# A two-layer recurrent kernel on one core: the last sequence's value projection moved behind the experts, and two orders swapped

## The chip, the cores and the metric

The kernel runs on one core of a Trainium2 chip. The metric is device time in microseconds (us) of one execution, as the median over runs.

## What is computed

The input is eight sequences of 512 tokens with 128 features, float32. Layer 0 normalises each token, runs causal attention with two query heads and one shared key/value head, and a mixture of eight experts of which each token takes two; the output is x + attention * silu(experts). Layer 1 (a causal convolution, a gated running state, a small memory product and a gated feed-forward) follows on the same rows. Cut to what the change touches:

```python
xn = _layernorm(x)
k = apply_rope(xn @ Wk.T);  v = xn @ Wv.T;  q = apply_rope(einsum(xn, Wq))
w = softmax(where(causal, q @ k.T * scale, -inf))
s = (w @ v) @ Wo.T                      # attention, two heads
g = silu(experts(xn))                   # 8 experts, each token takes the best two
x = x + s * g                           # then layer 1 on x
```

## The kernel before, in words

The kernel names every instruction and orders each engine's queue by hand; engines meet at counting semaphores.

**Order of the stages.** First the normalisation and the router; then attention of sequences 0 to 6; then the experts over 71 tiles of 128 slots (the tokens have been scattered into slots sorted by expert); then attention of sequence 7, for which queries and keys were made before the experts; then layer 1, sequence by sequence. Only the last attention lies between the experts and layer 1.

**Attention of one sequence** (attend, NS = 8 steps, one for each pair of a block of 128 query rows and a head, in the order of STEPS). In step k TensorE does scores(k) (two float32 passes and a small bf16 matmul that adds the causal mask, lines 804 and 806), turn(k-1) (transposes of the exponentials, line 820) and weigh(k-2) (their product with the values, line 842). VectorE takes the row maximum (row_max, line 1330), ScalarE the exponential with its row sum (exponent, line 1796) and copies the transposed tile out of its bank (turned, line 1805), VectorE inverts the row sum (line 1335). For the even outputs ScalarE scales the head-0 product (head0, line 1814), and VectorE adds head 1 to it (combine, line 1323). A weigh of head 1 waits for the head0 copy that reads the same bank. Each engine runs its list in order, so an instruction that waits holds up all that stand behind it.

**Projections of the next sequence** sit in the same steps, at the steps of PROJECT_AT: parts 0 to 2 are queries and keys (line 785) with the rotation on VectorE (lines 1301 to 1313); part 3 is the value projection, four 128x256 products (eight passes, line 792), into banks 1 and 0. ScalarE copies these banks into U with two copies (values, lines 1766 and 1767). For sequence 7, part 3 stands at step 7 of attention 6, and its copies in finish(6), between turned(7) and head0(3). proj_full counts the projections, proj_free the banks that are free again; the experts start once proj_free has reached 4 * (NB + 1) = 32, which includes these copies.

**Experts** (c_step). Per tile TensorE does the gate (line 928), the up (line 937) and, for the tile before, the down product (line 946); ScalarE the gelu (line 1895) and a copy of the next up weights (line 1821); VectorE transposes the next tile's tokens (c_turn, line 1380), forms the product (line 1425), and for the tile before adds the bias (line 1399) and scales into YO (c_out, line 1408). GpSimd scatters YO to rows_y in DRAM (c_send, line 637), two buffers in turn; so c_out(j) waits until the scatter of tile j-2 has landed (c_st). GpSimd's first scatter waits for the slots' tags, which it casts at line 633. SyncE's queue loads the gate weights (line 452) and the token tiles (line 477).

**Last attention.** attend(NB, first=True, last=True), the first of a new pipeline. At step 1 TensorE waits for the last YO and runs keep_warm(0, 5), five 128x512 bf16 matmuls whose result nobody reads (line 736). When all scatters have landed, SyncE issues 16 loads of 256 KB (line 509): for each sequence, the rows of both choices of expert, into Y0 (over XR) and Y1 (over XNT, the normalised input transposed). VectorE starts layer 1 within this attention: d_first_both (line 1463, the sum of the two rows of sequence 0) in step 4 behind row_max and the reciprocal, d_first_product (line 1467) in step 5, d_first_gate with d_add_x (lines 1472, 1502) in step 6, d_stats(0) in step 7. ScalarE's tanh of those sums (d_tanh, line 1930) stands at the end of steps 4 and 6.

Of the kernel before, what the change touches and what calls it, by code (L numbers as in the profile page):

```python
# [27 lines left out]
NSEQ, SEQ = 8, 512  # L28
# [32 lines left out]
def stores(u):  # L61

    return (SLOT_TILES + 1 - u) // 2


NB = NSEQ - 1
# [3 lines left out]
PROJECT_AT = [(1, 3, 5, 7), (1, 4, 6, 7)]  # L70
# [14 lines left out]
def build(nc, t, out):  # L85
    ctx = ExitStack()
    with ctx:
# [3 lines left out]
        def sem(name):  # L91
            return ctx.enter_context(nc.semaphore(name))
# [224 lines left out]
        proj_full = sem("proj_full")  # L317
        proj_free = sem("proj_free")
# [102 lines left out]
        def _(sp):  # L421
# [83 lines left out]
            for u in range(2):  # L505
                sp.wait_ge(c_st[u], 16 * stores(u))
            for b in range(NSEQ):
                for k, y in ((0, Y0), (1, Y1)):
                    sp.dma_start(y[:, b * TPS:(b + 1) * TPS, :], rows_y_t[:, k, b * TPS:(b + 1) * TPS, :]
                                 ).then_inc(rows_in[b], 16)  # L510
# [219 lines left out]
        def _(pe):  # L730
# [3 lines left out]
            def keep_warm(bank, times):  # L734
                for _ in range(times):
                    pe.matmul(B[bank][:].rearrange("p (a b) -> p a b", b=P), ONB[:],
                              ONB[:, None, :].broadcast_to([P, 4, P]), start=True, stop=True)
# [108 lines left out]
            def count():  # L846

                pe.wait_ge(r_m, 1)
                pe.wait_ge(proj_free, 4)
                pe.matmul(B[1][:, NT * E:2 * NT * E], ONB[:], MB, start=True, stop=True)  # L850
                pe.matmul(B[1][:, 0:NT * E], lowb, MB, start=True, stop=True).then_inc(r_cnt, 1)

            def attend(b, u, first=False, last=False):
                for k in range(NS):
                    scores(b, u, k)
                    if b == 0 and k == 1:
                        project(0, 0, 3)
                        turn(0, 0)
                        composite(1)
                        count()  # L860
                    if b == 0 and k == 2:
                        composite(2)
                    if not last and k in PROJECT_AT[b == 0]:
                        project(b + 1, 1 - u, PROJECT_AT[b == 0].index(k))
                    if last and k == 1:
                        pe.wait_ge(c_yo, SLOT_TILES)
                        keep_warm(0, 5)
                    if not (first and k < 1) and not (b == 0 and k == 1):
                        turn(b if k >= 1 else b - 1, (k - 1) % NS)
                    if not (first and k < 2):  # L870
                        weigh(b if k >= 2 else b - 1, u if k >= 2 else 1 - u, (k - 2) % NS)
# [89 lines left out]
                    pe.reg_load(e_down, TEXP[0:1, bass.ds(j - 1, 1)])  # L961
                    c_down(j - 1, 1 - u, pe.snap(e_down, min_val=0, max_val=E - 1))

            pe.wait_ge(proj_free, 4 * (NB + 1))
            for j in range(WBUFS):
                c_step(j, j % 2, j)
            with pe.Fori(1, C_ROUNDS) as i:
# [206 lines left out]
        def _(dve):  # L1174
# [152 lines left out]
            def row_max(b, k):  # L1327
                i, _ = STEPS[k]
                dve.wait_ge(s_full, NS * b + (k + 1))
                dve.tensor_reduce(NM[:, k:k + 1], B[2 + k % 2][:, 0:(i + 1) * P], AX.X, ALU.max,  # L1330
                                  negate=True).then_inc(max_done, 1)
# [4 lines left out]

            def attend(b, u, first=False, last=False):
                for k in range(NS):
                    row_max(b, k)
                    if b == 0 and k == 1:  # L1340
                        choose(1)
                        mark(1)
                    if not (first and k == 0):
                        denominator(b if k else b - 1, (k - 1) % NS)
                    if b == 0 and k == 2:
                        offsets()
                    if b == 0 and k == 3:
                        gates()
                    if last and k == 4:
                        d_first_both()  # L1350
                    if last and k == 5:
                        d_first_product()
                    if k in (5, 6):
                        combine(b, k - 5)
                    if k in (1, 2) and not first:
                        combine(b - 1, k + 1)
                    if k in ROPE_AT[b == 0] and not last:
                        rope_begin(b + 1, ROPE_AT[b == 0].index(k))
                    if k - 1 in ROPE_AT[b == 0] and not last:
                        rope_end(b + 1, 1 - u, ROPE_AT[b == 0].index(k - 1))  # L1360
                    if b == 1 and k in (1, 3, 5):
                        experts((k - 1) // 2)
                    if last:
                        if k == 6:
                            d_first_gate()
                        if k == 7:
                            d_stats(0)
# [93 lines left out]
            def d_first_both():  # L1461
                dve.wait_ge(rows_in[0], 16 * 3)
                dve.tensor_tensor(Y0[:, 0:TPS, :], Y0[:, 0:TPS, :], Y1[:, 0:TPS, :], ALU.add).then_inc(d_mo, 1)
# [261 lines left out]
        def _(act):  # L1725
# [38 lines left out]
            def values(b, u):  # L1764
                act.wait_ge(proj_full, 4 * b + 4)
                act.activation(U[u][:, 0:2, :], B[0][:].rearrange("p (i d) -> p i d", i=2), ACT.Copy)
                act.activation(U[u][:, 2:4, :], B[1][:].rearrange("p (i d) -> p i d", i=2), ACT.Copy
                               ).then_inc(proj_free, 1)
# [30 lines left out]
            def turned(b, k):  # L1799
                i, _ = STEPS[k]  # L1800
                n = NS * b + k
                act.wait_ge(t_done, n + 1)
                if not (isinstance(b, int) and n < 2):
                    act.wait_ge(pv_done, n - 1)
                act.activation(PT[k % 2][:, 0:(i + 1) * P], B[4 + k % 2][:, 0:(i + 1) * P], ACT.Copy  # L1805
                               ).then_inc(pt_done, 1)

            def head0(b, c):
                k = {0: 0, 1: 1, 2: 4, 3: 5}[c]
                n = NS * b + k  # L1810
                act.wait_ge(pv_done, n + 1)
                act.wait_ge(rd_done, n + 1)
                reg = B[6 + k % 2][:, 0:P]
                act.activation(O0[c], reg, ACT.Copy, scale=RD[:, k:k + 1]).then_inc(o0_done, 1)  # L1814
# [14 lines left out]
            def attend(b, u, first=False, last=False):  # L1829
                for k in range(NS):  # L1830
                    if k in (3, 4):
                        head0(b, k - 3)
                    if k == 7:
                        head0(b, 2)
                    if k == 0 and not first:
                        head0(b - 1, 3)
                    if b == NB - 1 and k == 6:
                        first_up_weights(0, e_this)
                    if b == NB - 1 and k == 7:
                        first_up_weights(1, e_next)  # L1840
                    exponent(b, k)
                    if isinstance(b, int) and b == 0 and k == 1:
                        values(0, 0)
                    if not (first and k == 0):
                        turned(b if k else b - 1, (k - 1) % NS)
                    if isinstance(b, int) and b == 0:
                        if k in (1, 2):
                            composite(k)
                        if k == 1:
                            counted()  # L1850
                        if k == 2:
                            exponents()
                        if k >= 4 and k - 4 + KEPT < TAPS:
                            j = k - 4 + KEPT
                            act.activation(TAPW[:, k - 4, :], W3[:, 2, :], ACT.Copy,
                                           scale=VEC[:, V_CONV + j:V_CONV + j + 1]).then_inc(w_am, 1)
                    if last:
                        if k == 4:
                            d_tanh(0)
                        if k == 6:  # L1860
                            d_tanh(1)
                if not last and b != NB - 1:
                    values(b + 1, 1 - u)

            def finish(b):
                turned(b, NS - 1)
                if b == NB - 1:
                    values(b + 1, 1 - b % 2)
                head0(b, 3)
                bring_table(ACT.Gelu if b < NSEQ - 1 else ACT.Silu)  # L1870

            def counted():
# [280 lines left out]
```

## Time and profile before

| what | value |
|---|---|
| median of three runs | 527.14 us (527.08 to 527.35) |
| the profiled execution | 528.09 us, of which its span 526.2 us |
| TensorE matmul busy | 512.3 us, 97% of the span |
| VectorE, ScalarE, GpSimd busy | 390.9, 314.0, 234.6 us |
| attention 6 ends, experts start | at 157.85 us of the span |
| last attention starts | at 348.95 us |

The profile is of one execution; times below are from the start of its span. A row of a timeline gives the start, the duration, the engine, the line and the tile written and read, how many instructions are merged, and in brackets how long the engine sat idle before it and what released it. Durations of matmuls overlap: a float32 product is two passes, and the next pass starts before the modelled end of the one before.

### The profile page before, as it was taken

Reading aid. Unit: us, or ns where it says so; the run is one execution under the profiler, and the core shown is the slowest. Engines: PE = TensorE matmul, PEld = TensorE weight load, DVE = VectorE, ACT = ScalarE, POOL = GpSimd, SP = SyncE. Lnnn points to the kernel's source line nnn. Section 1 sums busy time; section 2 is a strip of 40 time slices with the busy share of each in tenths; the row PEclk is TensorE's granted clock in tenths of the full one; section 3 lists DMA queues with packets and bytes.
Section 4 is the critical chain, followed back from the end, with each engine's and each line's share of the span. In section 5 each row is a group of like instructions: output and inputs, shape, how many; then the busy total and the mean of one; then the engine's idle time right before and its main releaser. Section 6 shows DMA issues by size and latency. Waiting matters only on the chain. (4 is left out here: it accounts for less than half of the span.)

```text
span 526.2 us, 12857 instructions
## 1 busy us (share of the span) xinstructions
PE 512.3 (97%) x3181; PEld 385.9 (73%) x3182; DVE 390.9 (74%) x1107; ACT 314.0 (60%) x830; POOL 234.6 (45%) x244
## 2 busy tenths in 40 slices
PE   9998999999999999999999999998999999999997
PEld 5756677777769999999999999976445545554544
DVE  6589878887776777677777777757788788788654
ACT  5635556556567666666666666657876657656521
POOL 4427766665532333333333333334477646523310
PEclk9999999999999999999999999999999999999999
DMA  8920133345429656555555566419000000000000
GB/s 238 379 109 22 42 102 106 100 127 172 141 43 124 149 146 152 146 149 142 156 137 155 135 152 147 122 55 285 7 0 20 16 5 21 21 0 21 21 19 22
DMA packets 85267, 54.00 MB, mean 103 GB/s; under 512 B 53088, under 2 KB 70016, under 8 KB 85104
## 3 DMA queue, kind: packets, MB, share of 16 engines
q1 hardware_dynamic: 80912, 44.66, 33.7%
q0 software_dynamic: 4320, 8.92, 4.7%
q8 instruction: 16, 0.26, 0.2%
q14 instruction: 19, 0.16, 0.1%
HBM read 37.82 MB, written 15.74 MB: 102 GB/s over the span
## 5 line engine op out<-in xcount | busy, mean ns | idle before, releaser
L1895 ACT ACTIVATE AR<-bank,BGT 128x128 f32<-128x128 f32 x284 | 81.3, 368 | 69.3 <-PE bank L928 69.3
L637 POOL DMA_INDIRECT rows_y<-YO,W1E x71 | 69.0, 972 | 118.6 <-DVE YO L1408 115.4
L1425 DVE SCALAR_TENSOR_TENSOR AR<-bank,B1T,AR 128x128 f32<-128x128 f32 x284 | 80.1, 344 | 3.7 <-ACT AR L1895 2.5
L601 POOL DMA_INDIRECT slots_x<-XR,SLOT x64 | 63.8, 996 | 36.5 <-DMA slots_x<-XR,SLOT 19.9
L946 PE MATMUL bank<-W2E,AR 128*128 x568 | 75.1, 275 | 0.5 <-DVE AR L1425 0.5
L928 PE MATMUL bank<-AR,WGE 128*128 128x128 f32 x568 | 75.1, 275 | 0.0
L937 PE MATMUL bank<-AR,WGE 128*128 128x128 f32 x568 | 75.0, 275 | 0.0
L946 PEld LDWEIGHTS bank<-W2E,AR 128*128 128x128 f32 x568 | 69.1, 192 | 0.7 <-issue 0.7
L937 PEld LDWEIGHTS bank<-AR,WGE 128*128 128x128 f32 x568 | 69.2, 192 | 0.0
L928 PEld LDWEIGHTS bank<-AR,WGE 128*128 128x128 f32 x568 | 69.1, 192 | 0.0
L1796 ACT ACTIVATE AR<-bank,AR 128x512 f32<-128x512 f32 (+1 forms) x64 | 33.8, 528 | 54.0 <-DVE AR L1330 54.0
L842 PE MATMUL bank<-AR 128*128 128x128 f32 x320 | 47.9, 280 | 1.9 <-ACT AR L1814 1.0
L1380 DVE STREAM_TRANSPOSE AR<-XG 128x128 f32<-128x128 f32 x71 | 22.1, 311 | 35.6 <-PE bank L937 27.8
L1330 DVE TENSOR_REDUCE AR<-bank 128x1 f32<-128x512 f32 (+1 forms) x64 | 31.0, 487 | 20.2 <-PE bank L806 19.8
L1821 ACT ACTIVATE WGE<-SPARE 128x512 f32 x71 | 45.5, 641 | 0.3
L804 PE MATMUL bank<-AR 128*128 128x128 f32 (+3 forms) x128 | 45.1, 435 | 0.0
L842 PEld LDWEIGHTS bank<-AR 128*128 128x128 f32 x320 | 40.7, 191 | 5.0 <-ACT AR L1805 3.3
L820 PEld LDWEIGHTS bank<-CST,AR 128*128 128x128 f32 x160 | 19.2, 140 | 23.0 <-ACT AR L1796 11.2
L2027 ACT ACTIVATE W1E<-bank 128x512 f32<-128x512 f32 x32 | 19.0, 593 | 26.9 <-PE bank L1070 26.9
L1070 PE MATMUL bank<-WGE,WGT 128*128 128x512 f32 x64 | 32.7, 593 | 0.7 <-DVE X L1636 0.7
L1076 PE MATMUL bank<-WGE,WUP 128*128 128x512 f32 x64 | 32.7, 592 | 0.0
L1588 DVE SCALAR_TENSOR_TENSOR SPARE<-W2E,VEC,SPARE 128x512 f32<-128x512 f32 x35 | 31.7, 905 | 1.1
(217 smaller groups left out, 907.6 us busy)
## 6 DMA issues: line engine op xcount, KB each, us to landing
WGE<-in_wgu SPq DMA_DIRECT2D x71, 256.0 KB
XG<-slots_x SPq DMA_DIRECT2D x140, 32.0 KB
slots_x<-W1E SPq DMA_DIRECT2D x7, 585.0 KB, 7.3
X<-in_x SPq DMA_DIRECT2D x8, 256.0 KB, 5.6
SPARE<-in_wgu SPq DMA_DIRECT2D x8, 256.0 KB, 2.8
W2E<-in_w SPq DMA_DIRECT2D x8, 256.0 KB, 3.2
XR<-rows_y SPq DMA_DIRECT2D x8, 256.0 KB, 5.3
XNT<-rows_y SPq DMA_DIRECT2D x8, 256.0 KB, 5.4
```

Source lines behind the costliest of these rows:

```text
L601: pool.indirect_dma_start(out=slots_x, out_offset=bass.IndirectOffsetOnAxis(ap=SLOT[:, k, n:n + 1], axis=0), in_=XR[:, n, :], in_offset=No ...
L637: pool.indirect_dma_start(out=rows_y, out_offset=bass.IndirectOffsetOnAxis(ap=DST[:, j:j + 1], axis=0), in_=YO[q % 2][:], in_offset=None). ...
L804: pe.matmul(bank[:, 0:(i + 1) * P], QT[u][h][:, i * P:(i + 1) * P], QT[u][2][:, 0:(i + 1) * P], start=True, stop=False)
L842: mm = pe.matmul(reg, PT[k % 2][:, j * P:(j + 1) * P], U[u][:, j, h * P:(h + 1) * P], start=(j == 0), stop=(j == i))
L928: mm = pe.matmul(B[1 + u][:, c * P:(c + 1) * P], WB[:, q, c * P:(c + 1) * P], XT[u], start=True, stop=True)
L937: mm = pe.matmul(B[3 + u][:, c * P:(c + 1) * P], WU[:, u, c * P:(c + 1) * P], XT[u], start=True, stop=True)
L946: mm = pe.matmul(B[5 + u][:, 0:P], HT[u][:, c, :], W2E[:, bass.ds(e, 1), c, :], start=(c == 0), stop=(c == FC - 1))
L1070: pe.matmul(B[5 - 3 * (c % 2)][:], WGT[:, c * P:(c + 1) * P], H2, start=True, stop=True).then_inc(d_g, 1)
L1425: s = dve.scalar_tensor_tensor(out=HT[u][:, c, :], in0=B[3 + u][:, c * P:(c + 1) * P], scalar=B1T[:, bass.ds(e, 1), c], in1=ZB[u][:, c, :] ...
L1796: act.activation(PR[k % 2][:, 0:(i + 1) * P], B[2 + k % 2][:, 0:(i + 1) * P], ACT.Exp, bias=NM[:, k:k + 1], accum_out=DEN[:, k:k + 1]).the ...
L1821: act.activation(WU[:, u:u + 1, :], SPARE[:, bass.ds(e, 1), :], ACT.Copy).then_inc(c_wu, 1)
L1895: act.activation(ZB[u][:, c, :], B[1 + u][:, c * P:(c + 1) * P], ACT.Gelu, bias=BGT[:, bass.ds(e, 1), c]).then_inc(c_gelu, 1)
```

## The change

TensorE leaves out the last projection of attention 6 and does it in step 1 of attention 7, in place of the five warm matmuls. The experts wait for one count less. ScalarE copies the values in step 1 of attention 7, behind the exponent and ahead of turned(0); in finish(6), head0(3) now stands ahead of turned(7). VectorE's d_first_both moves from behind row_max(4) and the reciprocal to ahead of them. SyncE waits for the last projection before it loads the rows of sequence 7 over XNT.

```diff
@@ sync @@
             for b in range(NSEQ):
+                if b == NSEQ - 1:
+                    sp.wait_ge(proj_full, 4 * NSEQ)
                 for k, y in ((0, Y0), (1, Y1)):
@@ tensor, attend @@
-                    if not last and k in PROJECT_AT[b == 0]:
+                    if not last and k in PROJECT_AT[b == 0] and not (b == NB - 1 and k == 7):
                         project(b + 1, 1 - u, PROJECT_AT[b == 0].index(k))
                     if last and k == 1:
+                        project(b, u, 3)
                         pe.wait_ge(c_yo, SLOT_TILES)
-                        keep_warm(0, 5)
@@ tensor, experts @@
-            pe.wait_ge(proj_free, 4 * (NB + 1))
+            pe.wait_ge(proj_free, 4 * NB + 3)
@@ vector, attend @@
                 for k in range(NS):
+                    if last and k == 4:
+                        d_first_both()
                     row_max(b, k)
...
-                    if last and k == 4:
-                        d_first_both()
@@ scalar, attend and finish @@
                     exponent(b, k)
-                    if isinstance(b, int) and b == 0 and k == 1:
-                        values(0, 0)
+                    if isinstance(b, int) and b in (0, NB) and k == 1:
+                        values(b, u)
...
             def finish(b):
+                if b == NB - 1:
+                    head0(b, 3)
                 turned(b, NS - 1)
-                if b == NB - 1:
-                    values(b + 1, 1 - b % 2)
-                head0(b, 3)
+                if b == NB:
+                    head0(b, 3)
                 bring_table(ACT.Gelu if b < NSEQ - 1 else ACT.Silu)
```

## Rows read from the trace of the kernel before

**Rows 1.** The page, busy time and share of the span by engine

```profile
PE 512.3 (97%) x3181; PEld 385.9 (73%) x3182; DVE 390.9 (74%) x1107; ACT 314.0 (60%) x830; POOL 234.6 (45%) x244
```

**Rows 2.** Timeline of TensorE at the end of attention 6: start, duration, engine, line

```profile
152.24 2.24 PE L792 MATMUL bank<-CVO,XNT 128*128 128x256 f32 x8
154.32 0.49 PE L820 MATMUL bank<-CST,AR 128*128 128x128 f32 x3
...
155.39 0.94 PE L842 MATMUL bank<-AR 128*128 128x128 f32 x6
157.33 0.68 PE L842 MATMUL bank<-AR 128*128 128x128 f32 x4 [1.00 <-ACT AR L1814]
157.85 1.06 PE L928 MATMUL bank<-AR,WGE 128*128 128x128 f32 x8
```

**Rows 3.** Timeline of ScalarE in the same stretch

```profile
154.40 0.47 ACT L1796 ACTIVATE AR<-bank,AR 128x256 f32<-128x256 f32 x1 [0.50 <-DVE AR L1330]
...
154.86 0.48 ACT L1805 ACTIVATE AR<-bank 128x384 f32<-128x384 f32 x1
155.56 0.39 ACT L1805 ACTIVATE AR<-bank 128x256 f32<-128x256 f32 x1 [0.22 <-PE bank L820]
155.85 0.59 ACT L1766 ACTIVATE AR<-bank 128x512 f32<-128x512 f32 x1
...
156.80 0.38 ACT L1814 ACTIVATE AR<-bank,AR 128x128 f32<-128x128 f32 x1
```

**Rows 4.** Timeline of VectorE around the output of expert tile 2

```profile
168.17 0.28 DVE L1399 TENSOR_TENSOR YB<-bank,B2E 128x128 f32<-128x128 f32 x1
168.68 0.29 DVE L1408 TENSOR_SCALAR YO<-YB,W1E 128x128 f32<-128x128 f32 x1 [0.23 <-DMA rows_y<-YO,W1E]
169.63 0.31 DVE L1380 STREAM_TRANSPOSE AR<-XG 128x128 f32<-128x128 f32 x1 [0.66 <-issue]
```

**Rows 5.** Timeline of GpSimd: the first and the last scatter of expert rows

```profile
164.26 1.00 POOL L637 DMA_INDIRECT rows_y<-YO,W1E  x1 [0.61 <-POOL W1E L633]
...
350.23 0.97 POOL L637 DMA_INDIRECT rows_y<-YO,W1E  x1 [0.57 <-DVE YO L1408]
```

**Rows 6.** Timeline of TensorE: the gate product of expert tile 5

```profile
170.39 1.06 PE L928 MATMUL bank<-AR,WGE 128*128 128x128 f32 x8
```

**Rows 7.** Timeline of SyncE's queue: the first two loads of rows

```profile
352.48 0.39 SPq L509 DMA_DIRECT2D XR<-rows_y  x1
352.91 0.51 SPq L509 DMA_DIRECT2D XNT<-rows_y  x1
```

**Rows 8.** Timeline of TensorE in the last attention

```profile
350.20 1.24 PE L736 MATMUL bank<-ONB 128*128 128x512 bf16 x5
351.86 0.66 PE L820 MATMUL bank<-CST,AR 128*128 128x128 f32 x4 [0.42 <-ACT AR L1796]
...
353.38 1.06 PE L842 MATMUL bank<-AR 128*128 128x128 f32 x8
...
355.03 0.66 PE L820 MATMUL bank<-CST,AR 128*128 128x128 f32 x4 [0.31 <-ACT AR L1796]
```

**Rows 9.** Timeline of ScalarE in the last attention

```profile
352.55 0.60 ACT L1805 ACTIVATE AR<-bank 128x512 f32<-128x512 f32 x1 [0.40 <-PE bank L820]
354.20 0.69 ACT L1796 ACTIVATE AR<-bank,AR 128x512 f32<-128x512 f32 x1 [1.05 <-DVE AR L1330]
...
357.24 0.58 ACT L1796 ACTIVATE AR<-bank,AR 128x384 f32<-128x384 f32 x1 [0.67 <-DVE AR L1330]
```

**Rows 10.** Timeline of VectorE in step 4 of the last attention

```profile
356.65 0.56 DVE L1330 TENSOR_REDUCE AR<-bank 128x1 f32<-128x384 f32 x1 [1.48 <-PE bank L806]
...
357.19 0.67 DVE L1463 TENSOR_TENSOR XR<-XR,XNT 128x512 f32<-128x512 f32 x1
```

**Rows 11.** The loads of rows, issue to landing: the first two, then all 16

```profile
DMA to landing us min/median/max: 3.3/3.5/3.8
...
DMA to landing us min/median/max: 3.3/5.4/5.7
```

## The prediction, made before the changed kernel was run

> **What bounds the kernel now.** I read the page's busy times first: TensorE is busy for 97% of the span [rows 1], and the other three are far below. A change of order can win or lose only where TensorE stands still, or by the passes it drops or adds. So I went on to TensorE's timeline at the two seams that the change touches, and from each of its waits to the engine that ended it. At the first seam TensorE idles 1.00 us ahead of the last weigh of attention 6, until ScalarE's head0 copy (line 1814) has read the bank [rows 2]; ScalarE had put the two value copies ahead of that copy [rows 3]. At the second seam, in the last attention, TensorE waits 0.42 us for the first exponential, which is after the five warm matmuls, and 0.31 us for the third [rows 8]. Then I followed what a seam that is earlier runs into: a VectorE instruction that waits for a scatter [rows 4, 5], and the first loads of expert rows [rows 7, 11].
>
> All sums are against the profiled execution, 528.09 us with a span of 526.2, and what they give is carried over to the median of 527.14. A measurement of this kernel can tell about 0.2%, 1.05 us, from no change.
>
> **Leaving attention 6.** The eight passes of line 792 run from 152.24 to the next instruction at 154.32: 2.08 us go from TensorE [rows 2]. They free nothing by themselves. ScalarE's exponential of step 7 starts at 154.40 on VectorE's row maximum, and turned(6) right behind it at 154.86 [rows 3]; neither waits for the projection, so the six passes of weigh that need turned(6) still start at 155.39 [rows 2]. What follows is shorter. Behind turned(6), which ends at 155.34, head0(3) (0.38 us) goes first, as its product is then long made, to about 155.6; turned(7) already starts at 155.56 when nothing is ahead of it and takes 0.39 us [rows 3], so it ends near 155.95. The six passes hand over at about 156.05 (their end of 156.33 less the overlap of 0.16 to 0.3 that modelled ends have here), and the last weigh follows at 156.08 in place of 157.33 [rows 2]. **TensorE reaches the experts 1.25 us earlier**, at 156.60 in place of 157.85. The new wait of the experts asks only for the rotated keys and queries, done before. The gelu table is loaded behind turned(7), 1.2 us earlier too, and stays hidden behind the first gate product of 1.06 us plus the up product.
>
> **What that earlier start collides with.** VectorE's c_out(2) (line 1408) waits for the scatter of tile 0 to land, since both use one YO buffer. It was already a little late: idle 0.23 us, released by that DMA at 168.68 [rows 4]. The scatter was issued at 164.26, as soon as GpSimd had cast the tags [rows 5]; the tags come by a DMA that starts from the end of the token scatter and not from TensorE, so this time doesn't move. Nor does its queue: SyncE issues those loads one behind the other without a pause there. Queued behind c_out(2) on VectorE is c_turn(5), which starts at 169.63 and takes 0.31 us [rows 4], and TensorE's gate product of tile 5 needs it: 170.39 before [rows 6], 169.14 wanted now. With the 0.15 us that lie between a VectorE end and the matmul, it starts at 169.94 + 0.15 = 170.09. **So 0.30 us of the 1.25 is left.** Afterwards VectorE's step is no longer than TensorE's, and nothing is won back. The bounds: 1.25 if the scatter lands earlier than the row suggests, and 0 if that VectorE chain slips as well. I take 0.30, by rows 4 and 6.
>
> Rows 5 and 7 give the same scatter without other traffic: issued at 350.23, its landing released SyncE at 352.48, 2.25 us; the loaded one took up to 168.68 - 164.26 = 4.4 us. The Trainium skill (DMA: Bandwidth & Descriptors, "Anatomy of one DMA — SWDGE (gpsimd) path") puts such a DMA at about 2.0 us fixed plus bytes over 436 GB/s. The unloaded scatter agrees with it and the loaded one does not; by the page the scatter would land near 166.4, c_out(2) would wait for nothing, and the full 1.25 us would stay.
>
> **Entering the last attention.** The projection takes the place of the warm matmuls at 350.20. It costs 2.08 us until the next instruction, so turn(0) starts at 352.28 in place of 351.86 (it was waiting for the exponential) [rows 2, 8]: **+0.42 us**. The other path is ScalarE. The projection's modelled end is 350.20 + 2.24 = 352.44; the two copies start at about 352.5 and hold ScalarE for 156.80 - 155.85 = 0.95 us [rows 3]. turned(0) starts at about 353.47 in place of 352.55 and takes 0.60 [rows 9], so the first weigh starts near 354.13 in place of 353.38 [rows 8]: +0.75. Behind it TensorE had 0.31 us of slack before turn(2) at 355.03 [rows 8], which leaves 0.44. The third exponential (354.20, released by a row maximum [rows 9]) comes 0.42 later, by turn(0). Both paths say that TensorE is 0.42 to 0.45 us later from step 3 on. SyncE's new wait for the projection costs nothing: it ends near 352.4, and SyncE comes to sequence 7 only as its last pair of 16 loads, the first of which is issued at 352.48 [rows 7].
>
> **Row sums ahead of row_max(4).** VectorE was idle for 1.48 us before row_max(4) at 356.65, and d_first_both took 0.67 us behind it [rows 10]. In front it would be free if its rows were there. They are not: the second load of sequence 0 is issued at 352.91 and takes 3.8 us [rows 7, 11], so they are complete at 356.71. d_first_both runs from about 356.80, and row_max(4), 0.62 us behind it (the pitch of a 0.67 us instruction), at 357.42. Without the move it would start at 356.65 + 0.43 = 357.08. So the step is late by 357.42 - 356.65 = **0.77 us in all**, the 0.43 included. The exponential of step 4 starts 0.59 us behind its row maximum (357.24 before [rows 9, 10]), TensorE's next transposes wait for it, and VectorE's chain into layer 1 (row_max(6), the gate, row_max(7), the statistics) hangs on it in turn. I find no slack behind it that gives any back. The bounds: 0.42 if the rows come before 356.3, and about 1.5 if they come 0.7 us later.
>
> **Sum:** -0.30 + 0.77 = +0.47 us. The profiled execution would give 528.56, the median 527.6.
>
> **Rivals.**
> The full gain at the first seam: the scatter has in truth landed well before 168.68 and the row's 0.23 us is mostly the pause before every line 1408. For it: the page's rule above, and an unloaded landing of 2.25 us. Against: the wait is put down to the DMA by name. Then -1.25 + 0.77 = -0.48, 526.66 us, no change that can be told.
> Faster: that full gain, and in the last attention the delays are swallowed, because the rows of sequence 0 come early and the added wait on ScalarE falls into the 0.42 and 0.31 us in which TensorE waited anyway. At most 0.2 us are then lost: -1.05 or better, 526.1 us. Against: the 2.08 us of passes alone take more than the 1.24 us of warm matmuls and their pause [rows 8].
> Slower, by one mechanism: d_first_both is a wait for a DMA at the head of VectorE's queue, with row_max(4) behind it, and behind that ScalarE and TensorE. Each microsecond by which the rows land after 356.71 is a microsecond of the kernel. It decides from 0.6 us late on (0.47 + 0.6 = 1.07), a flight of 4.4 us. At the median flight of all 16 loads, 5.4 us [rows 11], the rows land 1.6 us later and the time is 527.14 + 0.47 + 1.6 = 529.2. Against: the long flights are of the loads that queue behind others, and this is the second of all.
>
> **How the numbers follow.** My forecast (+0.47, 527.6) gets 0.56, the full gain at the first seam 0.22, both within 1.05 us of before: same 0.78. The faster case gets 0.07, the slower one 0.15. The range goes down to 526.5 (the full gain, -0.48, and a little of the slack in the last attention) and up to 528.4 (the rows 0.8 us late), which leaves out most of the faster case and the far half of the slower one.
>
> **What would show it.** Right: no line 792 between 152 and 154.4, and line 928 at about 156.6; line 1408 of tile 2 with an idle time near 1.4 us put down to the scatter, and the gate product of tile 5 near 170.1; in the last attention eight passes of line 792, the first weigh 0.75 us later against the start of the attention, and line 1463 behind an idle time that the load of XNT ends, about 7.85 us after the attention's start at 348.95, with line 1330 right behind. Wrong: an expert stage that starts and ends 1.25 us earlier, a line 1463 that waits for nothing, or a TensorE that is back in its old rhythm by step 7. A granted clock below full speed anywhere in the last attention, now that the warm matmuls are gone, would also prove me wrong.

## The result, and the profile after

The changed kernel takes 529.35 us in the median of 20 runs, the kernel before 527.42 in 20 runs beside it. Executions of 534 us and more, in which the granted clock of TensorE is at half for 17 us early in the load phase (seen in the profiles of e1 and i3 below), are left out of the ratio: five here and three before, without which the medians are 528.92 and 527.35. The ratio is 1.0022, interval [1.0012, 1.0032]. That is 1.16 us slower (0.0022 x 527.42; 0.6 to 1.7 by the interval), just past what can be told from no change. The forecast was 527.6, in a range of 526.5 to 528.4. The profiled execution took 528.12 us (528.09 before) with the same span of 526.2 us, so the totals of the two traces show nothing of this; they have to be cut into stretches.

The page, busy times (against [rows 1]):

```profile
PE 511.1 (97%) x3176; PEld 385.8 (73%) x3177; DVE 391.4 (74%) x1107; ACT 313.5 (60%) x830; POOL 233.9 (44%) x244
```

The totals tell nothing. Four stretches do, cut by starts in the timelines: **seam 1** from the last exponential of attention 6 to the first gate product; **experts** from there to the first scores of the last attention; **attention** from there to the first transposes of layer 1; **layer 1** from there to the end. In us, for every kernel profiled here (* a fallen clock, below):

```
kernel                          seam 1  experts  attention  layer 1
before                           3.45   191.11    17.80     159.43
changed                          2.22   191.15    19.82     159.44
e1 row sums back                 2.22   192.03    18.74     159.43
e2 row sums alone                3.45   191.68    19.18     159.43
e3 head copy alone               2.62   192.08    17.81     159.44
e4 warm matmuls in step 5        2.22   191.37    19.93     159.43
f1 GpSimd's sum held             2.22   191.92    19.23     159.44
f2 projection alone              2.45   191.37    18.41     159.43
f3 third buffer, sums back       2.99*  191.97*   18.46     159.09
f4 head copy + third buffer      2.62   191.17    17.80     159.10
g1 warm matmuls in step 7        2.22   192.10    20.10     159.43
g2 changed once more             2.22   191.88    20.64     159.43
g3 g1 + sums back                2.22   192.78    18.47     159.44
h1 row loads paced               2.22   191.90    19.53     159.45
h2 h1 + f1                       3.12*  192.20*   19.58     159.44
i1 6 waits on SyncE              2.22   191.47    19.76     159.45
i2 16 waits on SyncE             2.22   192.14    20.55     159.43
i3 16 waits on TensorE           2.22   191.65    18.75     159.44
i4 16 waits on ScalarE           3.08*  191.83*   19.84     159.45
```

The changed kernel wins 1.23 us at seam 1 and loses 2.02 in the last attention. The spans are equal because everything ahead of seam 1, where nothing was changed, ran 0.80 us shorter in this execution (the last exponential starts at 153.60 and not at 154.40 [rows 3]).

Seam 1, timeline of TensorE and then of ScalarE, the kernel after:

```profile
152.10 0.55 PE L822 MATMUL bank<-CST,AR 128*128 128x128 f32 x3 [0.50 <-ACT AR L1798]
154.22 0.44 PE L822 MATMUL bank<-CST,AR 128*128 128x128 f32 x2 [1.12 <-ACT AR L1798]
154.60 1.38 PE L844 MATMUL bank<-AR 128*128 128x128 f32 x10
155.81 1.06 PE L930 MATMUL bank<-AR,WGE 128*128 128x128 f32 x8
```

```profile
153.60 0.47 ACT L1798 ACTIVATE AR<-bank,AR 128x256 f32<-128x256 f32 x1 [0.50 <-DVE AR L1332]
154.06 0.48 ACT L1807 ACTIVATE AR<-bank 128x384 f32<-128x384 f32 x1
154.43 0.37 ACT L1816 ACTIVATE AR<-bank,AR 128x128 f32<-128x128 f32 x1
154.69 0.38 ACT L1807 ACTIVATE AR<-bank 128x256 f32<-128x256 f32 x1
```

The six and the four passes of weigh, apart before [rows 2], now stand in one row of ten: the wait of 1.00 us for the head copy is gone. (The lines of the kernel after are numbered two higher: 822 is the transposes, 844 weigh, 930 the gate, 1382 c_turn, 1410 c_out, 1465 and 1469 the row sum and the product, 511 the row loads.) The projection's time shows as two waits instead, 0.50 and 1.12 us, which cost nothing here. The collision that was foreseen, on VectorE and then on TensorE:

```profile
165.05 0.31 DVE L1382 STREAM_TRANSPOSE AR<-XG 128x128 f32<-128x128 f32 x1 [0.76 <-DMA XG<-slots_x]
...
166.88 0.29 DVE L1410 TENSOR_SCALAR YO<-YB,W1E 128x128 f32<-128x128 f32 x1 [0.28 <-DMA rows_y<-YO,W1E]
167.82 0.31 DVE L1382 STREAM_TRANSPOSE AR<-XG 128x128 f32<-128x128 f32 x1 [0.66 <-PE bank L939]
```

```profile
168.36 1.06 PE L930 MATMUL bank<-AR,WGE 128*128 128x128 f32 x8
```

The scatter was issued at 163.27 and released line 1410 at 166.88: 3.6 us, not the 4.4 of before. The gate product of tile 5 stands 12.55 us behind the first one, as before (170.39 - 157.85 = 12.54 [rows 2, 6]): no loss in this execution, and the idle time before line 1410 is 0.28 us where 1.4 was foreseen. The Trainium skill (DMA: Bandwidth & Descriptors, "Anatomy of one DMA — SWDGE (gpsimd) path") would have it land after some 2.15 us; this row does not agree either.

The last attention, timelines of TensorE, VectorE, GpSimd and SyncE's queue, the kernel after:

```profile
348.21 1.95 PE L794 MATMUL bank<-CVO,XNT 128*128 128x256 f32 x8
349.99 0.60 PE L822 MATMUL bank<-CST,AR 128*128 128x128 f32 x4
...
351.82 1.16 PE L844 MATMUL bank<-AR 128*128 128x128 f32 x8 [0.20 <-ACT AR L1807]
...
353.10 0.66 PE L822 MATMUL bank<-CST,AR 128*128 128x128 f32 x4
...
357.60 0.55 PE L822 MATMUL bank<-CST,AR 128*128 128x128 f32 x3 [1.33 <-ACT AR L1798]
```

```profile
355.68 0.69 DVE L1465 TENSOR_TENSOR XR<-XR,XNT 128x512 f32<-128x512 f32 x1 [2.02 <-DMA XNT<-rows_y]
356.29 0.55 DVE L1332 TENSOR_REDUCE AR<-bank 128x1 f32<-128x384 f32 x1
...
357.66 1.68 DVE L1469 TENSOR_TENSOR SA<-XR,SA 128x512 f32<-128x512 f32 x1
```

```profile
357.52 1.27 POOL L693 TENSOR_TENSOR XR<-XR,XNT 128x512 f32<-128x512 f32 x1 [7.67 <-DMA XNT<-rows_y]
```

```profile
350.91 0.51 SPq L511 DMA_DIRECT2D XNT<-rows_y  x1
351.46 0.51 SPq L511 DMA_DIRECT2D XR<-rows_y  x1
...
353.11 1.69 SPq L511 DMA_DIRECT2D XNT<-rows_y  x1
```

The attention starts at 346.96. Up to step 3 TensorE is only 0.06 us late: turn(2) at 6.14 us from the start, 6.08 before (355.03 - 348.95 [rows 8]). Then VectorE stands for 2.02 us in front of the row sum, with the row maximum right behind it, and TensorE for 1.33. The row sum starts 8.72 us from the start (355.68 - 346.96); foreseen was 7.85. And a product of 0.67 us takes 1.68, while GpSimd's sum of 1.27 us runs beside it.

### The profile page after: what moved, and what is told of

The parts are those of the page before. It is cut to its first block and busy times, and to the rows that moved or that the text cites. A ratio compares the mean times of both kernels' runs of the same rounds, so it can differ in the third digit from the quotient of the medians.

```text
span 526.2 us, 12847 instructions
## 1 busy us (share of the span) xinstructions
PE 511.1 (97%) x3176; PEld 385.8 (73%) x3177; DVE 391.4 (74%) x1107; ACT 313.5 (60%) x830; POOL 233.9 (44%) x244
## 5 line engine op out<-in xcount | busy, mean ns | idle before, releaser
L822 PE MATMUL bank<-CST,AR 128*128 128x128 f32 x160 | 28.6, 277 | 4.2 <-ACT AR L1798 4.2
```

Source lines behind the costliest of these rows:

```text
L822: mm = pe.transpose(B[4 + k % 2][:, j * P:(j + 1) * P], PR[k % 2][:, j * P:(j + 1) * P], ident)
```

## The experiments

**One part undone, one part alone.**

e1, the row sums put back:

```diff
                 for k in range(NS):
-                    if last and k == 4:
-                        d_first_both()
                     row_max(b, k)
...
+                    if last and k == 4:
+                        d_first_both()
```

> The changed kernel with the sum of the two expert rows (line 1465 of after) put back behind row_max(4) and the reciprocal. Theory W (a wait on the rows' DMA holds up VectorE's queue): the idle time of 2.02 us before that sum and TensorE's 1.33 us before the transposes of step 5 go, the last attention from its first scores to the first transposes of layer 1 takes 18.2 to 18.5 us (17.8 before, 19.8 in the changed kernel), and the kernel is 0.7 to 1.2 us faster than the one before, since the first seam keeps its 1.2 us. Rival L (the moved value copies are what makes the attention late): it stays above 19.3 us and the kernel stays no faster than before.

Measured: ratio 1.0023 [0.9992, 1.0053], which decides nothing: two of the eleven runs in it took 534.3 and 534.9 us. The other nine have a mean of 527.94 us, against 527.96 for the kernel before, so the 0.7 to 1.2 us that were expected did not come; the expert stage took 0.92 us more in the profile. Attention 18.74 us, 0.24 over the upper end: the second load took longer in this profile than in all but one of the others (g2), and VectorE waited 0.88 us for it even with the row sums behind row_max(4). Theory W holds against L: 1.1 us of the 2.02 go with the order of the row sums.

e2, the opposite edit, in the kernel before:

> The kernel before with only the row sums moved ahead of row_max(4). Theory W: rows of sequence 0 are complete 4 to 4.7 us after the second load is issued, VectorE stands still until then, and the last attention takes 1.0 to 1.7 us longer than the 17.8 of before; the kernel is 1.0 to 1.7 us slower. Rival L: under 0.4 us.

Measured: attention 19.18 us, 1.38 longer. The order of the row sums alone costs that in the profile. The runs show 0.6 us (1.0011 [1.0000, 1.0022]), less than the 1.0 to 1.7 expected.

e3, in the kernel before:

```diff
             def finish(b):
+                if b == NB - 1:
+                    head0(b, 3)
                 turned(b, NS - 1)
                 if b == NB - 1:
                     values(b + 1, 1 - b % 2)
-                head0(b, 3)
+                if b == NB:
+                    head0(b, 3)
```

> The kernel before with only the head-0 copy of finish(6) moved ahead of turned(7); the values stay where they were. The last weigh no longer waits for the value copies (its wait falls from 1.0 us to near 0), but the experts still wait for them: they end at about 157.2 instead of 156.9 (line 1814 now ahead), so the experts start at about 157.3 instead of 157.85, 0.4 to 0.6 us faster. If the move of the projection alone carries the gain, this one gives under 0.2 us.

Measured: seam 1 2.62 us, 0.83 shorter, more than expected: two thirds of the change's gain come from the order of two ScalarE instructions. Ratio 0.9992 [0.9980, 1.0005], no change that can be told; the expert stage took 0.98 us more in its profile.

f2, the projection and its copies moved, both orders as before:

> Only the projection and its copies moved: row sums back behind row_max(4), head-0 copy of finish(6) back behind turned(7). From the last exponential of attention 6 to the first gate product of the experts: 3.40 us before, 2.60 with the head copy alone, 2.20 with both. With the copies gone from between, the head-0 copy ends near 1.8 us after the exponential's start and the last weigh follows: 2.4 to 2.5 us. So the parts do not add up (0.8 and 0.9 give 1.2). The last attention takes 18.2 to 18.7 us.

Measured: 2.45 us and 18.41 us, both inside; 1.0000 [0.9986, 1.0014]. The move wins 1.00 at seam 1 and gives back 0.61 in the last attention. Most of that is the rows again: the second load took 5.0 us, and VectorE waited 0.54 us for it behind row_max(4), where it waited for nothing before. With the head copy's order in place already, the move wins only 0.40 more (2.62 to 2.22), less than it gives back.

**The overlap with GpSimd.** f1:

```diff
-            pool.wait_ge(d_mo, 1)
+            pool.wait_ge(d_sg, 1)
             both(1)
```

> The changed kernel, with GpSimd's sum of the rows of sequence 1 (line 693) held until VectorE's product of sequence 0 (line 1469) is done. In the changed kernel that product takes 1.68 us in place of 0.67 while GpSimd's sum runs beside it. Theory P (the two engines slow each other on SBUF, and VectorE's product is on the path): the product takes 0.67 us again, TensorE's wait of 0.45 us for line 1325 goes, and the last attention is 0.4 to 1.0 us shorter than the 19.8 us of the changed kernel (18.8 to 19.4). Rival: the product is slow for another reason or has slack, and the attention stays at 19.7 to 19.9 us.

Timelines of VectorE and GpSimd in f1:

```profile
357.96 0.69 DVE L1465 TENSOR_TENSOR XR<-XR,XNT 128x512 f32<-128x512 f32 x1 [1.83 <-DMA XNT<-rows_y]
...
359.93 0.67 DVE L1469 TENSOR_TENSOR SA<-XR,SA 128x512 f32<-128x512 f32 x1
```

```profile
360.69 1.26 POOL L693 TENSOR_TENSOR XR<-XR,XNT 128x512 f32<-128x512 f32 x1 [8.38 <-DVE SA L1469]
```

The product is back at 0.67 us. From the start of the row sum to the end of the attention it is 10.70 us here (8.53 to 19.23) and 11.10 in the changed kernel (8.72 to 19.82): the overlap costs 0.40 us of its 1.0. Theory P holds, in profiles; the runs don't resolve it. Ratio 1.0006 [0.9989, 1.0022].

**What eats the gain in the expert stage.** f3 gives tile 0 an output buffer of its own, in e1; f4 does so in e3 (VectorE's write for tile 0 goes to it too, not shown):

```diff
+        YOF = sb("YOF", [P, P])
...
-                    in_=YO[q % 2][:], in_offset=None).then_inc(c_st[q % 2], 16)
+                    in_=(YOF if j == 0 else YO[q % 2])[:], in_offset=None).then_inc(c_st[q % 2], 16)
...
-                if not (isinstance(j, int) and j < 2):
+                if not (isinstance(j, int) and j < 3):
                     dve.wait_ge(c_st[u], (j - u) * 8)
```

> The changed kernel with the row sums back behind row_max(4) and a YO buffer of its own for tile 0, so that VectorE's output of tile 2 no longer waits for the scatter of tile 0. If that scatter is what eats the gain of the first seam: no idle time put down to the scatter at line 1411 for tile 2, and the expert stage takes 191.1 to 191.2 us in every profile (191.15 before, 192.03 and 192.10 in two runs). Rival: the token tiles 4 and 5, which queue behind the tags, hold up the gate product of tile 4 by themselves, and the stage still takes up to 191.8 us. Last attention 18.2 to 18.7 us; in time 0.5 to 1.0 us faster than before.

> The kernel before with the head-0 copy of finish(6) moved and a YO buffer of its own for tile 0; projection, values and row sums stay. First seam 2.6 us (3.40 before), expert stage 191.1 to 191.8 us, last attention 17.8 us as before: 0.3 to 0.8 us faster than before, and at least as fast as the version with the projection moved and the sums back, if the second seam gives back what the projection's move gains (0.4 us).

Measured: f3 0.9982 [0.9971, 0.9994], 0.9 us faster than before; f4 0.9974 [0.9961, 0.9987], 1.4 us faster and the best of all. In both profiles the wait for the scatter is gone, and in f4 the expert stage takes 191.17 us. The rival was right too, though: where the tags came later, it is the tokens of tile 4 that are late. In g3, VectorE and then TensorE:

```profile
168.67 0.31 DVE L1385 STREAM_TRANSPOSE AR<-XG 128x128 f32<-128x128 f32 x1 [2.69 <-DMA XG<-slots_x]
```

```profile
169.12 1.15 PE L933 MATMUL bank<-AR,WGE 128*128 128x128 f32 x8 [1.39 <-DVE AR L1385]
```

That wait on TensorE appears in e1, e3, f1, g1, g2, g3, h1 and i2 (0.44 to 1.39 us), in all of which GpSimd's cast of the tags comes 7.0 us or more behind the first gate product; in the others it comes after 4.5 to 6.8 us. In f3 and f4 it came early (4.5 and 4.8), so they do not tell whether the third buffer helps where the tags are late. Part of the gain of f3 and f4, 0.33 us in both, lies in layer 1, where nothing was edited; this is not explained.

**The clock.** f3 missed its 2.2 us at seam 1. Windows there: the stretch and its length, TensorE's busy us (and instructions), its granted clock, DMA share and GB/s:

```profile
152.00:154.00 2.00, 0.94 (x7) 1.00 0.49 49
154.00:156.00 2.00, 1.95 (x11) 0.70 0.55 35
156.00:158.00 2.00, 2.00 (x11) 0.50 1.41 20
158.00:160.00 2.00, 2.00 (x19) 0.95 1.01 17
```

TensorE falls to 1.2 GHz from about 155 to 158 us, just behind the two waits that the projection has left. It costs some 0.8 us on seam 1 (2.99 against 2.22) and as much on the first expert products (191.97 against 191.17 in f4). e4 and g1 put warm matmuls back at two places, g1 so:

```diff
+                    if isinstance(b, int) and b == NB - 1 and k == 7:
+                        pe.wait_ge(proj_free, 4 * NB + 2)
+                        keep_warm(1, 9)
```

> The changed kernel with the five warm matmuls (bank 0) in step 5 of the last attention, inside TensorE's 1.33 us wait ahead of the transposes. They take 1.1 us and fit into the wait. Theory W: the time is that of the changed kernel within 0.3 us. Rival C (the dropped warm matmuls let the granted clock fall in some runs, which would explain runs of the changed kernel at a mean clock of 0.995 to 0.997 and 529.5 to 530.6 us): such runs vanish, and the median falls by 1 us or more.

> The changed kernel with nine warm matmuls (bank 1, 1.94 us) in step 7 of attention 6, where the value projection stood. One profile so far (of another variant with the projection moved) shows the granted clock at 0.50 for some 3.4 us from about 154.6 us on, just behind the two waits of 0.50 and 1.1 us in which TensorE now stands still there, and cost 0.8 us each on two stages; the changed kernel's runs fall in two groups, 528.1 to 528.6 and 528.9 to 530.6. Theory C (the projection had kept TensorE busy, and without it the clock falls in some runs): with the warm matmuls the upper group disappears but for what the kernel before has too, the median falls by 0.7 to 1.2 us against the changed kernel on the same chip, and the first seam stays at 2.2 to 2.3 us. Rival: the groups come from the load phase at the start alone; median and spread stay those of the changed kernel.

> The changed kernel once more, beside the others on the same chip. Segments: first seam 2.20 us if the clock holds, 3.0 if it falls; expert stage 191.15 to 192.1; last attention 19.8 to 20.0. Theory C: about half of the runs lie 1 to 2 us above the lower group.

> The changed kernel with the nine warm matmuls in step 7 of attention 6 and the row sums back behind row_max(4): the move of the projection without its two side effects. First seam 2.2 us, last attention 18.4 us, so -1.2 + 0.6 = -0.6 us and up to 0.9 us lost again in the expert stage: 0 to 0.6 us faster than before, and 1.2 to 1.6 us faster than g1. If theory C is false it differs from e1 by nothing.

Measured: e4 1.0027 [1.0014, 1.0040], no gain, and the clock fell in the last attention in none of the 19 profiles. g1 1.0015 [1.0002, 1.0027] with a median of 528.86, g2 1.0016 [1.0001, 1.0031] with 529.21, g3 0.9995 [0.9982, 1.0008], which like the changed kernel has a run of 530.3. So the expected fall of 0.7 to 1.2 us in the median did not come, and theory C does not explain the upper group of runs. The event is real but rare: the clock fell at seam 1 in 3 of 13 profiles with the projection gone (f3, h2, i4), in none of the 2 with warm matmuls in step 7 and none of the 4 with the projection in place. Six profiles without the event say too little for a rate. The mean granted clock on record for the runs says more: one fall of 3.4 us takes it to 0.997 (f3, e2). Among the runs below 533 us of the kernels measured repeatedly it is at or below that in 25 of 146 with the projection in place, in 32 of 95 with it gone and in 4 of 22 with warm matmuls in step 7. This agrees with more falls where the projection is gone, but it doesn't tell where in the execution they lie; at some 1.6 us each, a difference of one run in six is worth 0.3 us in the mean, too little for the groups. Other falls, in e2, e3, f1 and g3 at 24 to 28 us and in e1 and i3 before 35 us, are in the load phase, ahead of everything that was changed.

**Why the rows land later.** The second load took 3.8, 4.1, 4.4 and 4.0 us in the kernels with TensorE's and SyncE's lists as before (before, e2, e3, f4) and 4.5 to 5.6 in those with the projection moved up to then. h1 holds SyncE behind the first pair, h2 adds f1's edit:

```diff
+                if b == 1:
+                    sp.wait_ge(max_done, NS * NB + 3)
                 for k, y in ((0, Y0), (1, Y1)):
```

> The changed kernel, with SyncE held between the two loads of sequence 0 and the rest until the row maximum of step 2 is taken, some 5.3 us after the attention's start (third load 0.8 us later than in the changed kernel). In the profiles with SyncE's queue unchanged, the third or fourth load takes 1.2 to 1.5 us to issue, and the second load lands 3.8, 4.0, 4.1, 4.4 us after its issue; in those with the changed queue the third and fourth issue at once and it lands after 4.5 to 5.6 us. Theory Q (the loads behind it share the DMA engines with it, and the accidental pause had shielded it): the flight falls to 3.8 to 4.2 us, line 1467 starts at 7.8 to 8.2 us, and the last attention takes 18.9 to 19.3 us (its start plus 11.1) in place of 19.8 to 20.6. Rival: the flight has another cause (the projection reading XNT, an instruction fetch) and stays at 4.5 to 5.6 us.

> The same with GpSimd's sum of sequence 1 held until VectorE's product is done, so that both things that the prediction did not have are taken away. Theory: line 1467 starts at 7.8 to 8.2 us and the attention takes that plus 10.7, 18.5 to 18.9 us, which is the 18.57 of the prediction. Rival: a third cost is left and it stays above 19.2 us.

SyncE's queue in h1:

```profile
351.84 0.51 SPq L513 DMA_DIRECT2D XNT<-rows_y  x1
353.19 0.36 SPq L513 DMA_DIRECT2D XR<-rows_y  x1
```

The pause is there (1.35 us in place of 0.55), but the load still takes 4.6 us (h2: 4.9). Theory Q has fallen: the loads behind it are not what makes it late. h1 1.0021 [1.0001, 1.0041], h2 1.0007 [0.9994, 1.0019]. In h2 the attention takes 19.58 us, the row sum starts at 8.88, and 8.88 + 10.70 = 19.58: flight and overlap account for all of it, no third cost is left.

What does go with the flight is one 16 KB packet of the instruction queue. It was in the windows 352.8 to 353.8 us of before and 352.8 to 353.8 of after, which are 3.85 to 4.85 and 5.84 to 6.84 us from the attention's start. The queue of the row loads and that of the instructions, before first, then after:

```profile
q1 hardware_dynamic: 42, 0.02, 7.2%
q8 instruction: 1, 0.02, 6.2%
```

```profile
q1 hardware_dynamic: 605, 0.30, 99.8%
q8 instruction: 1, 0.02, 6.7%
```

6.7% of 16 engines for 1 us is one engine for 1.07 us. In the kernel before, the packet comes when the loads' data have hardly begun to move; in the changed one it comes while all 16 engines are full with them. In every profile a load that takes SyncE 1.2 to 2.2 us to issue, in place of 0.5, starts within 0.4 us of the packet's start: the third before (1.19 us), the sixth after (1.69 us, at 353.11 above). Start of the packet from the start of the attention (to the 0.1 us below), and flight of the second load:

```
before 4.3, 3.8   e2 4.3, 4.1   f4 4.3, 4.0   e3 5.0, 4.4   h1 6.0, 4.6   f1 6.1, 4.5
changed 6.3, 4.8  g1 6.4, 5.0   h2 6.4, 4.9   e4 6.5, 4.9   f2, f3, g3 6.8, 5.0
e1 7.0, 5.3       g2 7.2, 5.6
```

The i-kernels put waits that are already met into one engine's list, to move that packet if it is that engine's fetch:

> The changed kernel with six waits that are already met in SyncE's list ahead of the row loads. In 15 profiles a single 16 KB packet of the instruction queue, some 1.0 to 1.2 us long on one DMA engine, starts between 4.3 and 7.2 us after the attention's start, and the second row load lands the later the later it comes: 4.3 gives 7.8 to 8.1, 5.0 gives 8.4, 6.0 to 6.1 gives 8.5 to 8.6, 6.3 to 6.5 gives 8.8 to 9.0, 6.8 gives 9.0, 7.0 gives 9.3, 7.2 gives 9.6. Theory F: the packet delays the load, and it is a fetch of SyncE's instructions (SyncE's one slow issue, 1.2 to 1.7 us, comes with it). Then six more instructions move it two or three loads earlier, to about 4.5 us, and the load lands at 7.8 to 8.2. If it is another engine's fetch it stays between 6.0 and 7.2 us.

> The same with sixteen such waits. Theory F with SyncE's fetch: the packet comes before the loads start (ahead of 4.5 us), the load lands at 7.8 to 8.1. Otherwise the packet stays at 6.0 to 7.2 us.

> The changed kernel with sixteen met waits in TensorE's list ahead of the last attention. If the packet is TensorE's instruction fetch it moves by more than 1 us (either way); if not it stays between 6.0 and 7.2 us. Either way the landing of the second load follows the packet by the table of the other runs (theory F).

> The changed kernel with sixteen met waits in ScalarE's list ahead of the last attention. If the packet is ScalarE's instruction fetch it moves by more than 1 us; if not it stays between 6.0 and 7.2 us. The landing of the second load follows the packet (theory F).

Measured, packet and flight: i1 6.0, 4.6; i2 5.9, 4.9; i4 6.1, 4.8; i3 3.9, 3.9. SyncE's and ScalarE's lists leave it where it was; with TensorE's it came 2.4 us earlier (2.0 counted from the issue of the loads), the load was back at 3.9 us, and the row sum started at 7.52. The last attention took 18.75 us, the shortest of all with the row sums in front. Of the 1.2 us by which its row sum is earlier, 0.8 are the shorter flight. The other 0.4 only move from one stretch to the next: the waits hold TensorE ahead of its first scores (1.37 us behind the last down product's start, in place of 0.99), while the loads are issued as before. The projection stands in i3 where it stands in the changed kernel, so its reads of XNT alone do not make the flight long.

That fits an instruction fetch of TensorE that occupies one of the DMA engines while the load waits for its last part. But it is one run, of 535.63 us (its clock fell early, as e1's did, and e1 has the packet at 7.0). Two executions of the same program, changed and g2, differ by 0.9 us in the packet and by 0.8 in the flight. And g1, which adds eighteen TensorE instructions and left the packet at 6.4, speaks against it. Whose fetch it is stays open, and that the packet causes the delay is argued, not shown. That a later packet goes with a longer flight holds in all 19 profiles but for 0.4 us.

## Why the prediction was wrong

- **Seam 1 was right.** 1.25 us foreseen, 1.23 measured, by the step named: head copy ahead, last weigh right behind the six passes.
- **The collision in the expert stage was right in kind and wrong as a sum.** The step "So 0.30 us of the 1.25 is left" took the loaded scatter's 4.4 us as fixed. It took 3.6 in the profile of after, and nothing was lost there; over the other profiles of kernels with a shorter seam 1 and two YO buffers, 0.3 to 1.7 us are lost, and where it is 0.8 or more, TensorE waits for a neighbour that I had not named: the tokens of tile 4, queued behind the tags. On average 0.8 us of the gain are lost there, near the 0.95 foreseen, but mostly for another reason: that is luck. (e2, whose seam 1 is as before, loses 0.57 us too.)
- **Entering the last attention, the projection was overpriced.** 0.42 to 0.45 us by step 3 were foreseen and 0.06 came: line 794 takes 1.78 us to the next instruction (348.21 to 349.99) and not 2.08, since the earlier one had waited on its way: its fifth pass, the first behind the wait for bank 0, starts 0.41 us behind the fourth and the sixth 0.32 behind that, in place of 0.22. The 0.61 us of f2 are mostly the later landing.
- **The failing step is "they are complete at 356.71".** The flight of 3.8 us was taken from one execution, and it was the shortest of all 19. It took 4.8 in the changed kernel and 5.6 in g2, the same program again. So the row sum started 0.87 us later than foreseen (8.72 against 7.85), and another 0.87 later in g2, where the attention took 0.82 us more. That is the mechanism of the slower rival, to which I gave 0.15: a DMA wait at the head of VectorE's queue, each microsecond of it paid by the kernel.
- **A term was missing.** By starting later, the row sum and the product behind it met GpSimd's sum: 0.40 us. Together 0.77 + 0.87 + 0.40 = 2.04 against 2.02 measured.
- Sum over the stretches: -1.23 + 0.04 + 2.02 + 0.01 = +0.84 us. For g2, the same program again, it is -1.23 + 0.77 + 2.84 = +2.38. The runs give +1.16 (0.6 to 1.7), between the two. A granted clock below full speed was to prove me wrong in the last attention; it fell elsewhere, at seam 1, in some executions.

## What to carry to other kernels

Before a wait for a DMA is put at the head of an engine's list, ask who is queued behind it, and price the flight by its spread over several executions, not by the one at hand; here a sum that was free behind the row maximum cost 1.4 us in front of it in the profile (0.6 in the runs). When an edit has several parts, run each alone: two thirds of the gain was the order of two ScalarE copies, and the version with only that and one more buffer (f4) is the fastest, at 0.9974 of the kernel before.

## What the runs showed of the hardware that was not expected

- A 128x512 addition on GpSimd (1.27 us) slows a 128x512 product on VectorE that runs beside it: the product takes 1.68 us in place of 0.67 (1.48 to 1.70 over the profiles where they meet), and GpSimd's sum its usual time.
- A 16 KB packet of the instruction queue holds one of the 16 DMA engines for about 1 us (0.96 to 1.5), and the later it comes, the longer the flight of a 256 KB load issued ahead of it: 3.8 us at 4.3 us from the attention's start, 5.6 at 7.2. SyncE's issue of a load at that time takes 1.2 to 2.2 us in place of 0.5.
- Met waits are not free: six on SyncE's list moved the second load from 3.95 to 4.22 us, sixteen to 4.52, some 0.04 us each; sixteen on TensorE's list held its first scores back by 0.38 us.
